# Graph attention: the softmax's scaling moved behind the aggregation, a shorter lag, splits on GpSimd

## The reference, cut to what matters

```python
h = (x @ W.T).reshape(n, heads, out_ch)
e = leaky_relu(a_src[src] + a_dst[dst], 0.2)
m = segment_max(e, dst, num_segments=n)
ex = exp(e - m[dst])
denom = segment_sum(ex, dst, num_segments=n)
alpha = ex / (denom[dst] + 1e-16)
out = segment_sum(alpha[:, :, None] * h[src], dst, num_segments=n)
...
h = relu(gat_layer(x, W1, ..., heads=8, out_ch=128, concat=True))
out = gat_layer(h, W2, ..., heads=1, out_ch=768, concat=True)
```

## Time and profile before

| | us |
|---|---|
| median of 3 runs | 1967.06 (1966.3 to 1967.81) |
| profiled execution, its own time | 1970.35 |
| its span | 1968.5 |
| PE busy | 1850.9 (94%) |
| DVE busy | 1292.1 (66%) |
| ACT busy | 934.7 (47%) |
| POOL busy | 150.5 (8%) |

### The profile page before, as it was taken

The page is one execution under the profiler, slowest core; times in us unless marked ns, Lnnn a source line. Parts: engine busy times, 40 slices in busy tenths (PEclk is TensorE's granted clock), DMA queues, the critical chain, the costliest instruction groups (busy, mean ns, idle before and its releaser), DMA issues.

```text
span 1968.5 us, 30877 instructions
## 1 busy us (share of the span) xinstructions
PE 1850.9 (94%) x12157; PEld 1753.9 (89%) x12158; DVE 1292.1 (66%) x2489; ACT 934.7 (47%) x1547; POOL 150.5 (8%) x127
## 2 busy tenths in 40 slices
PE   6987999999999999788789999999999999999998
PEld 5876789998899999787689999999999999999998
DVE  7997766555245556888865754456566667676886
ACT  2331223315125435878534232345555566666776
POOL 0000000003000022333100000000101001001010
PEclk9997999999999989899799999999999999999999
DMA  3110002101113112010131132255656567677795
GB/s 117 49 49 1 25 25 105 54 6 71 49 49 110 54 36 95 22 38 17 64 123 61 62 105 73 73 208 181 220 193 221 214 217 242 219 260 250 282 318 203
DMA packets 36844, 234.30 MB, mean 119 GB/s; under 512 B 5964, under 2 KB 7366, under 8 KB 14680
## 3 DMA queue, kind: packets, MB, share of 16 engines
q1 hardware_dynamic: 31366, 217.41, 31.1%
q0 software_dynamic: 2656, 8.99, 2.1%
q10 hardware_dynamic: 2674, 5.87, 0.8%
HBM read 221.91 MB, written 10.35 MB: 118 GB/s over the span
## 4 chain that ended last, share of the span: by engine, by line
PE 43%; issue 3%; DVE 3%; DMA 1%; ACT 1%; POOL 0%; ACTq 0%; POOLq 0%; DVEq 0%
PE bank L2755 8%; PE bank L341 7%; PE bank L342 7%; PE bank L343 7%; PE bank L2756 4%; PE bank L2767 3%; PE bank L2771 2%; PE bank L2759 2%; PE bank L2768 2%; PE bank L2770 1%; PE bank L2758 1%; DVE weight_lo L314 1%; DMA out<-ffn_y,slot_token 0%; PE bank L2713 0%; DMA weight_raw_fifth<-in_ffn_w 0%
## 5 line engine op out<-in xcount | busy, mean ns | idle before, releaser
L314 DVE TENSOR_TENSOR weight_lo<-weight_raw,weight_hi 128x2304 fp32r<-128x2304 f32 (+1 forms) x155 | 392.3, 2536 | 51.5 <-ACT weight_hi L304 51.4
L304 ACT ACTIVATE weight_hi<-weight_raw 128x2304 fp32r<-128x2304 f32 (+1 forms) x155 | 323.3, 2087 | 76.7 <-DMA weight_raw<-in_ffn_w 55.0
L341 PE MATMUL bank<-xT_hi,weight_hi 128*128 128x320 f32 (+1 forms) x576 | 183.2, 318 | 5.3 <-DVE xT_lo L362 5.2
L342 PE MATMUL bank<-xT_lo,weight_hi 128*128 128x320 f32 (+1 forms) x576 | 178.3, 310 | 0.0
L343 PE MATMUL bank<-xT_hi,weight_lo 128*128 128x320 f32 (+1 forms) x576 | 178.1, 309 | 0.0
L341 PE MATMUL bank<-weight_hi,xT_hi 128*128 128x384 f32 (+1 forms) x480 | 161.2, 336 | 11.2 <-DVE weight_lo L314 6.2
L3135 DVE TENSOR_TENSOR hidden_tmp<-hidden_tmp,bank 128x160 f32<-128x160 f32 (+5 forms) x192 | 65.6, 342 | 160.7 <-ACT hidden_tmp L2918 160.7
L342 PE MATMUL bank<-weight_lo,xT_hi 128*128 128x384 f32 (+1 forms) x480 | 157.0, 327 | 0.0
L343 PE MATMUL bank<-weight_hi,xT_lo 128*128 128x384 f32 (+1 forms) x480 | 156.7, 326 | 0.0
L613 PE MATMUL bank<-one_hot_dst,one_hot_src 125*128 125x313 f16 x800 | 123.5, 306 | 15.2 <-ACT packed_counts L627 7.9
L2918 ACT ACTIVATE hidden_tmp<-bank,ffn_b_by_load 128x160 f32<-128x160 f32 (+5 forms) x192 | 73.3, 402 | 117.5 <-PE bank L2759 112.8
(11 more groups left out here) (495 smaller groups left out, 5040.8 us busy)
## 6 DMA issues: line engine op xcount, KB each, us to landing
weight_raw<-in_ffn_w SPq DMA_DIRECT2D x111, 1152.0 KB, 5.2
weight_raw_fifth<-in_ffn_w SPq DMA_DIRECT2D x25, 1152.0 KB, 5.2
weight_raw<-in_shared_w SPq DMA_DIRECT2D x16, 1152.0 KB, 5.1
weight_raw<-in_mix_kv SPq DMA_DIRECT2D x8, 1152.0 KB, 7.0
weight_raw<-in_gat_w SPq DMA_DIRECT2D x8, 768.0 KB, 4.3
weight_raw<-in_mix_q SPq DMA_DIRECT2D x4, 1152.0 KB, 5.1
weight_raw<-in_mix_out SPq DMA_DIRECT2D x4, 1152.0 KB, 5.2
weight_raw<-in_gnn_w SPq DMA_DIRECT2D x4, 1152.0 KB, 5.6
```

The lines of the kernel that those rows point to most:

```text
L304: act.activation(upper_, whole_, ACT.Copy).then_inc(*w_hi.one())
L314: dve.tensor_tensor(lower_, whole_, upper_.bitcast(F32), ALU.subtract).then_inc(*w_lo.one())
L341: pe.matmul(dst, a[0], b[0], start=first, stop=False)
L342: pe.matmul(dst, a[0], b[1], start=False, stop=False)
```

## The change

- The exponentials are no longer multiplied by the inverse of their sum (L2253 and its three small DVE steps go). Instead, once for each pair, DVE adds `least_sum` to the sums and inverts them (2 small steps), PE spreads the inverses over all partitions by a transpose of a broadcast column for each tile, ACT copies that bank to `inverse`, and DVE multiplies the Z bank by it into `zt`. ACT then takes Relu in place in `zt` and writes the high part, at the end of its tick.
- The low part of z is a POOL subtraction in place of a DVE one.
- The lags shrink: turn 3 in place of 5, splits 4 in place of 6, Z 5 in place of 7. Z comes first in PE's tick, and multiplication, Relu and splits of z come in the same tick (before in the next one). The loop has 48 ticks in place of 50 (`LAST_LAG`).
- `PREPARE`, `Y_AT` and `SPLIT` are moved, `ZS` goes from 7 to 5, `zT` has three slots in place of two.

```diff
+        least_sum = sb("gat_least_sum", [P, TT], F32, gat)
-        ZS, XS = 7, DEPTH
+        ZS, XS = 5, DEPTH
-        zT = pair("gat_zT", [P, 2, 2, 2 * P], gat)
+        zT = pair("gat_zT", [P, 3, 2, 2 * P], gat)
+        inverse = count_f32[:, 2 * TP:2 * TP + 2 * P]
...
-        LAST_LAG = 10
+        LAST_LAG = 8
-        PREPARE = {6: (0, 1), 7: (2, 3), 8: (4,)}
-        Y_AT = {10 * grp + tick: (grp, t) for grp in range(4) for t, tick in enumerate((12, 13, 18, 19, 21) if grp < 3 else (12, 13, 16, 17, 18))}
+        PREPARE = {5: (0,), 6: (1,), 7: (2, 3), 8: (4,)}, {4: (0,), 5: (1, 2), 6: (3,), 7: (4,)}
+        Y_AT = {10 * grp + tick: (grp, t) for grp in range(4) for t, tick in enumerate({2: (12, 13, 16, 17, 18), 3: (10, 11, 14, 15, 16)}.get(grp, (12, 13, 18, 19, 21)))}
-        SPLIT = {10: c0 + 2, 12: c0 + 3, 14: c0 + 4, 20: c0 + 5, 24: c0 + 6, 28: c0 + 7}
+        SPLIT = {10: c0 + 2, 12: c0 + 3, 18: c0 + 4, 20: c0 + 5, 28: c0 + 6, 30: c0 + 7}
...
         def z_slot(q):
+            return pairs_of[q][2] // 2
+
+        def sums_before(q):
             grp, h, t0, n = pairs_of[q]
-            return (3 * grp + t0 // 2) % 2
-        def sums_after(q):
-            grp, h, t0, n = pairs_of[q]
-            return y_full.at(2 * (grp * TT + t0 + n))
+            return y_full.at(2 * ((grp - 1) * TT + t0 + n))
...
-            for u in range(N1):
-                terms(u, *units[u][0:3])
+            for i in range(N1 + LAST_LAG):
+                if i < N1:
+                    terms(i, *units[i][0:3])
+                q = pair_closing(i, 5)
+                if q is not None:
+                    grp, h, t0, n = pairs_of[q]
+                    hi, lo = at(zT, ALL, z_slot(q), h, slice(0, n * P))
+                    pool.wait_ge(*z_hi.at(q + 1))
+                    pool.tensor_tensor(lo, zt[:, q % 2, 0:n * P], hi.bitcast(F32), ALU.subtract).then_inc(*z_lo.one())
...
             for i in range(N1 + LAST_LAG):
+                q = pair_closing(i, 5)
+                if q is not None:
...
+                    bank = ring.next(z_scaled.at(q + 1))
...
                 if i in Y_AT:
...
-                q = pair_closing(i, 7)
...
-                    bank = ring.next(z_relu.at(q + 1))
...
-                u = unit(i, 5)
+                u = unit(i, 3)
                 if u is not None:
-                    turn_unit(u, e_scaled.at(u + 1))
+                    turn_unit(u, e_exp.at(u + 1))
+                q = pair_closing(i, 4)
+                if q is not None:
+                    grp, h, t0, n = pairs_of[q]
+                    pe.wait_ge(*e_summed.at(q + 1))
+                    bank = ring.next(inverse_kept.at(q + 1))
+                    inverse_banks.append(bank)
+                    for t in range(n):
+                        end = pe.transpose(bank[:, t * P:(t + 1) * P], total[:, grp % 2, h, t0 + t:t0 + t + 1].broadcast_to([P, P]), ident[:, :])
+                    end.then_inc(*inverse_full.one())
...
-                    act.activation(zt[:, q % 2, 0:n * P], z_banks[q][:, 0:n * P], ACT.Relu, bias=b1[:, 2 * grp + h:2 * grp + h + 1]).then_inc(*z_relu.one())
...
-                u = unit(i, 6)
+                u = unit(i, 4)
...
-                    act.wait_ge(*e_summed.at(u + 1))
-                    act.activation(e, e, ACT.Copy, scale=total[:, grp % 2, h, t:t + 1]).then_inc(*e_scaled.one())
+                q = pair_closing(i, 5)
+                if q is not None:
+                    n = pairs_of[q][3]
+                    act.wait_ge(*inverse_full.at(q + 1))
+                    if q:
+                        act.wait_ge(*z_scaled.at(q))
+                    act.activation(inverse[:, 0:n * P], inverse_banks[q][:, 0:n * P], ACT.Copy).then_inc(*inverse_kept.one())
...
                     raw_edges(u, *units[u][0:3])
+                q = pair_closing(i, 5)
+                if q is not None:
+                    grp, h, t0, n = pairs_of[q]
+                    act.wait_ge(*z_scaled.at(q + 1))
+                    z = zt[:, q % 2, 0:n * P]
+                    act.activation(z, z, ACT.Relu, bias=b1[:, 2 * grp + h:2 * grp + h + 1]).then_inc(*z_relu.one())
+                    act.wait_ge(*z_relu.now())
+                    if grp:
+                        act.wait_ge(*sums_before(q))
+                    upper(at(zT, ALL, z_slot(q), h, slice(0, n * P)), z).then_inc(*z_hi.one())
...
-                    lower(at(zT, ALL, z_slot(q), h, slice(0, n * P)), zt[:, q % 2, 0:n * P]).then_inc(*z_lo.one())
-                u = unit(i, 6)
+                u = unit(i, 4)
                 if u is not None:
                     turned_lower(u, at(exT, ALL, u % XS, ALL, ALL))
-                    dve.wait_ge(*e_exp.at(u + 1))
-                    own_step(dve.tensor_scalar(tot, tot, 1e-16, None, ALU.add))
-                    own_step(dve.reciprocal(tot, tot))
-                    dve.tensor_tensor(tot, tot, has_edge[:, t:t + 1], ALU.mult).then_inc(*e_summed.one())
...
                     peak(u, *units[u][0:3])
+                if pair_closing(i, 3) is not None:
+                    grp, h, t0, n = pairs_of[pair_closing(i, 3)]
+                    sums = total[:, grp % 2, h, t0:t0 + n]
+                    dve.wait_ge(*e_exp.at(i - 3 + 1))
+                    own_step(dve.tensor_tensor(sums, sums, least_sum[:, t0:t0 + n], ALU.add))
+                    dve.reciprocal(sums, sums).then_inc(*e_summed.one())
+                q = pair_closing(i, 5)
+                if q is not None:
+                    grp, h, t0, n = pairs_of[q]
+                    dve.wait_ge(*z_full.at(q + 1))
+                    dve.wait_ge(*inverse_kept.at(q + 1))
+                    if q >= 2:
+                        dve.wait_ge(*z_lo.at(q - 1))
+                    dve.tensor_tensor(zt[:, q % 2, 0:n * P], z_banks[q][:, 0:n * P], inverse[:, 0:n * P], ALU.mult).then_inc(*z_scaled.one())
```

More of the change, by code:

```diff
@@ L1954, in preparations @@
             if i < N1 and i // 10 < 3:
-                for step in PREPARE.get(i % 10, ()):
+                for step in PREPARE[i >= 10].get(i % 10, ()):
                     yield i // 10 + 1, step
@@ L2093, in tensor @@
             for i in range(N1 + LAST_LAG):
+                q = pair_closing(i, 5)
+                if q is not None:
+                    grp, h, t0, n = pairs_of[q]
+                    u = FIRST_OF[q]
+                    pe.wait_ge(*ex_lo.at(2 * (u + n)))
+                    pe.wait_ge(*h_lo.at(TT * (grp + 1)))
+                    bank = ring.next(z_scaled.at(q + 1))
+                    z_banks.append(bank)
+                    slots = slice(u % XS, u % XS + n) if u % XS + n <= XS else slice(u % XS, None, -(XS - 1))
+                    product(bank[:, 0:n * P].rearrange("p (a n) -> p a n", n=P),
+                            [(at(hg[grp % 2], ALL, k, slice(h * P, (h + 1) * P)), at(exT, ALL, slots, k, ALL)) for k in range(TT)]).then_inc(*z_full.one())
                 if i in Y_AT:
@@ L2104, in tensor @@
                                                   for k in range(2)]).then_inc(*y_full.one())
-                q = pair_closing(i, 7)
-                if q is not None:
-                    grp, h, t0, n = pairs_of[q]
-                    u = FIRST_OF[q]
-                    pe.wait_ge(*ex_lo.at(2 * (u + n)))
-                    pe.wait_ge(*h_lo.at(TT * (grp + 1)))
-                    bank = ring.next(z_relu.at(q + 1))
-                    z_banks.append(bank)
-                    slots = slice(u % XS, u % XS + n) if u % XS + n <= XS else slice(u % XS, None, -(XS - 1))
-                    product(bank[:, 0:n * P].rearrange("p (a n) -> p a n", n=P),
-                            [(at(hg[grp % 2], ALL, k, slice(h * P, (h + 1) * P)), at(exT, ALL, slots, k, ALL)) for k in range(TT)]).then_inc(*z_full.one())
                 if i in TURNED:
@@ L2196, in exponent @@
                 act.wait_ge(*e_made.at(u + 1))
+                if grp > 1 and t == 0:
+                    act.wait_ge(*aggregated(grp - 2))
                 act.activation(e, e, ACT.Exp, bias=minus_peak[:, grp % 2, h, t:t + 1], scale=-1.0,
@@ L2228, in scalar @@
                     act.dma_start(slots_dram[:, 0:D].rearrange("(t p) d -> p t d", p=P), x[:, :, :]).then_inc(*x_kept.dma())
-                q = pair_closing(i, 8)
-                if q is not None:
-                    grp, h, t0, n = pairs_of[q]
-                    act.wait_ge(*z_full.at(q + 1))
-                    if q >= 2:
-                        act.wait_ge(*z_lo.at(q - 1))
-                    act.activation(zt[:, q % 2, 0:n * P], z_banks[q][:, 0:n * P], ACT.Relu, bias=b1[:, 2 * grp + h:2 * grp + h + 1]).then_inc(*z_relu.one())
-                    act.wait_ge(*z_relu.now())
-                    if q >= 4:
-                        act.wait_ge(*sums_after(q - 4))
-                    upper(at(zT, ALL, z_slot(q), h, slice(0, n * P)), zt[:, q % 2, 0:n * P]).then_inc(*z_hi.one())
                 if i in Y_AT and Y_AT[i][1] == TT - 1:
@@ L2247, in scalar @@
```

(10 more changed lines are left out.)

18 lines of the change are left out of this document (6 added, 12 removed).

## The result

| | before | changed |
|---|---|---|
| median of 20 runs, us | 1967.91 | 1973.04 |
| profiled execution, its own time | 1970.35 | 1976.22 |
| its span | 1968.5 | 1974.4 |

The ratio of changed to before is 1.0022, with a 95% interval from 1.0012 to 1.0031: some 4 us slower (the medians are 5.1 us apart), where 11 us faster was forecast. The ratio is over fast runs alone, which leaves out one run of the kernel before that took 2981.48 us. The profiled execution of the changed kernel is 3.2 us above its own median.

The account below looks back on a forecast made before the run. The first GAT layer's loop was taken as bound by uneven ticks, with PE, DVE and ACT nearly equally loaded. Terms -15.0 + 1.5 + 3 - 2 + 1.5 = -11 us took the 1967.06 median to 1956, range 1946 to 1966.

Parts of the forecast that it names:

- The bound: First GAT layer's loop: PE, DVE and ACT nearly equally loaded, none full; bound by how unevenly the ticks load them.
- the same-tick chain: Pair ticks: DVE's multiplication waits for Z, ACT's Relu for the multiplication, with work queued behind; +3 us, bounds 0 and 8.
- The table of ticks: Loop ticks each priced by their most loaded engine: 170.5 us after against 185.5 before, so -15.0 us.
- The later weight splits: nothing: Moved `SPLIT` chunks stand two or more ticks ahead of the Y or projection reading them, so cost nothing.
- DVE against POOL: SBUF contention in the loop: -2 us for z's low part leaving DVE, +1.5 for peaks beside POOL's later terms.
- Rival C: POOL's terms wait behind z's low part, so DVE's peaks stand in all 24 pair ticks: +11 us, 1978; chance 0.08.
- The start: Loop's first ticks: PE's third turn needs banks held until DVE's additions for the last projection tiles; +1.5 us, bounds 0 and 2.2.
- Low part of z off DVE: Loop: 7 us of low-part work leaves DVE, plus -2 us counted for no longer standing beside POOL.
- ACT's relief: Loop: the scaling's 28.8 us goes; ACT's load falls from 149.2 to 130.6 us and ACT drops out as a bound.
- Two ticks of lag worth nothing: Loop start: PE begins turns behind the same projections, leaving 45 ticks in either kernel, so fewer lag ticks gain nothing.
- broadcast transposes as dear as others: PE's 40 transposes of inverses cost a fifth of a turn each, 0.094 us, together 3.8 us.
- the signs: Expected trace evidence, including L2253 gone, ACT's busy share of the loop down a fifth, loop 181 us, Relu's wait under 10.

Follow-up runs that it names:

- The best kernel: Changed kernel with ACT's Relu and z's high part in the next tick, POOL's low part a tick later, three weight splits one tick later; ratio 0.9948 to before.

## Why the prediction was wrong, point by point

**The bound** was read rightly: with all three engines loaded alike, placement decides. The best kernel does the same work as the changed one in another order and is 14.6 us faster (0.9948 against 1.0022), 10 us under the kernel before. That this is near the forecast of -11 is in part luck: without the two terms that its order takes away (the same-tick chain, +3, and POOL, +1.5) the prediction's sum is -15.5, and it stands at -10.2.

**The table of ticks** (-15.0, with the loop at 181 us and not the 198.6 measured) is the step that failed. It takes the longest engine of each tick, as if ACT's and DVE's work in a tick ran side by side. In a split tick they run one behind the other. For ticks 20 and 21 it gave 6.1 + 2.9 = 9.0 us, while PE's products of ticks 20 and 22 began at 849.17 and 860.38, 11.2 us apart. The 3% by which the table matched the kernel before did not vouch for it: that kernel has two stalls of this kind itself, 6.5 us together, against 13.0 in three after the change, and its level absorbed them. In the kernel before, moving the chunks gained nothing (1.0000), as another stall of 7.0 us came in their place. The table also takes PE's prices as fixed, while the Z behind the stall took 3.37 us and not 1.78.

**"The later weight splits: nothing"** was the sentence that hid it. I asked whether each chunk is ready for its reader. I did not ask who stands behind it in DVE's queue: the next turned tile's low part, and so Z. Undone, it gave 5 us (splits a tick later) and 4.5 us (Relu behind them).

**DVE against POOL**: the mechanism was forecast, and its place too, POOL's terms behind the subtraction beside the next peak. The size was not: +1.5 taken, bound +10, measured 5.5 by POOL's order alone. Rival C, which carried this to 26 us over all 24 pairs, had the sign right. By its own point (0.65 us a pair) it should not decide: the peaks over the loop were only some 5 us longer in the changed kernel, and its sign of over 1.2 us in most pair ticks held for six peaks. It needed the chunks' 5 us as well. I gave the combination no case of its own.
The rule named from the Trainium skill, page "SBUF — State Buffer", section "Who interferes with whom", is borne out for the peak, too: 1.52 us beside POOL's terms in place of 0.82.

**The same-tick chain** was taken at +3 with a bound of 8. As a wait it is far over what I named (31.7 us against "less than 10"), but most of it is idle time that costs nothing: with chunks and POOL moved the wait is still 29.0 us and the ratio 0.9971. What is left for Relu's place is the gap from 0.9971 to 0.9948, 4.5 us, with intervals that overlap. A reader who takes the largest new wait for the cause would have gone wrong here.

**The start**, +1.5: PE's third turn stood 2.31 us for the additions of the projection tiles, as described.

```profile
771.64 1.25 PE L2075 MATMUL bank<-identity,gat_edge 128*128 128x128 f32 x10
...
775.21 0.81 PE L2075 MATMUL bank<-identity,gat_edge 128*128 128x128 f32 x5 [2.31 <-DVE x L1839]
```

It was not undone by itself. **Low part of z off DVE**: 3.5 us, against 2 us of standing and the table's share of its 7 us of work. **ACT's relief**: the table said ACT drops out; 29 us put back cost 10 us. **Two ticks of lag worth nothing**, **broadcast transposes as dear as others**: the second is shown (282 against 274 ns), the first was not tried alone. Of the signs, ACT's busy share of the loop fell from 79% to 67%, a seventh and not a fifth. The range's ends, 1946 and 1966, are each 1 us below the working's 1947 and 1967, which changes nothing.

**The account**: -11 forecast, + 5 for the chunks, + 4 for POOL beyond the 1.5 counted, leaves -2, and +4.3 was measured. Of these 6 us, 1.5 may be Relu's place (4.5 against the 3 counted). The other 5 seem to lie outside the three placements: the best kernel, with all three undone, misses its sum of -15.5 by 5 us as well. That leaves the table's -15.0, the start's +1.5 and the -2 for the low part. The granted clock over the loop, 0.92 against 0.93, is worth 2 us at most (0.01 of 199). No run tells more, and this part stays open.

## What to carry to other kernels

A table of loads by stage is a floor, not a forecast: before it is believed, each long instruction must be asked what is queued behind it on its engine and on the engine that continues its work, and whether those two run one behind the other. When work moves to an idle engine, look at what that engine's queue holds behind the new wait, and which engine stands beside that work when it comes late. And a large new wait in the profile is a suspect only: here 29 us of waiting at one place cost some 4.5 us at the middle values, and perhaps less, while 13.6 us at another went with 5.

## What the runs showed of the hardware

DVE's peak, a custom instruction with two SBUF inputs, stands while POOL works on SBUF tiles: 1.24 us on average over 45 in the kernel with Relu last in its tick, 0.90 us when only POOL's order was changed. PE turns a broadcast column about as fast as a full tile (282 against 274 ns in the same loop). Behind a stall of 3.65 us its granted clock was 0.50, and the 15 matmuls of the next Z took 3.37 us in place of 1.78. On POOL a subtraction of 128x128 took 0.46 us and the terms of 128x640 1.56.
